# Node work of three graph convolutions and a final norm moved into the gather passes; matmul signals replaced by drains

## The reference

```python
def _gcn_conv(h, src, dst, norm, W, b, n_nodes):
    h = h @ W
    msg = h[src] * norm[:, None]          # norm = dinv[src] * dinv[dst]
    out = segment_sum(msg, dst, num_segments=n_nodes)
    return out + b
h = relu(_gcn_conv(x, src, dst, norm, W1, b1, n))
h = relu(_gcn_conv(h, src, dst, norm, W2, b2, n))
h = _gcn_conv(h, src, dst, norm, W3, b3, n)
x = layernorm(x + h)
```

## Time and profile before

| | us |
|---|---|
| median of 3 runs | 10497.17 (10493.28 to 10524.75) |
| the profiled execution | 10512.7 |
| its span | 10510.6 |

### The profile page before, as it was taken

How to read it: one execution, slowest core, us unless ns; L and a number is a source line. 1 busy time by engine, 2 the same in 40 slices (tenths; PEclk the granted TensorE clock), 3 DMA queues, 4 the chain that set the end, 5 groups by cost and what they waited for, 6 DMA issues and landing times. The chain is left out here.

```text
span 10510.6 us, 129336 instructions
## 1 busy us (share of the span) xinstructions
PE 6092.0 (58%) x27369; PEld 4863.8 (46%) x27370; DVE 4112.3 (39%) x9347; ACT 1787.8 (17%) x5309; POOL 5218.2 (50%) x5246
## 2 busy tenths in 40 slices
PE   3567666765675666667456533457854564455454
PEld 2456545644563555456334423345633443344343
DVE  5344434444453444434312523337761223224123
ACT  3222222222222222222323210001210000000000
POOL 2654454445446545644565445530036655655655
PEclk9788877877887888778778865558977787788777
DMA  5332332333233323323322145423313222222322
GB/s 149 108 94 86 98 102 84 98 90 103 83 93 103 96 85 98 105 84 89 92 82 79 32 138 165 148 97 131 114 60 88 83 71 86 85 80 72 87 78 70
DMA packets 423906, 995.27 MB, mean 95 GB/s; under 512 B 124608, under 2 KB 190016, under 8 KB 407360
## 3 DMA queue, kind: packets, MB, share of 16 engines
q0 software_dynamic: 246800, 677.71, 22.4%
q1 hardware_dynamic: 152608, 293.79, 8.5%
q10 hardware_dynamic: 24336, 22.16, 0.6%
HBM read 858.93 MB, written 134.35 MB: 95 GB/s over the span
## 5 line engine op out<-in xcount | busy, mean ns | idle before, releaser
L283 POOL DMA_INDIRECT ring<-node_table,idx x4608 | 4510.2, 979 | 3679.3 <-issue 1667.8
L250 DVE SCALAR_TENSOR_TENSOR S<-iota,block_start,dst_f 128x512 f32<-128x512 f32 x1900 | 1423.2, 749 | 3256.2 <-remote 1813.2
L497 PE MATMUL psAT<-ring,S 128*128 128x256 f32 x7600 | 2023.4, 426 | 1065.6 <-DVE AGG L614 917.8
L321 PE MATMUL psAT<-ring,S 128*128 128x256 f32 x6080 | 1709.1, 443 | 1506.2 <-DVE AGG L365 743.3
L497 PEld LDWEIGHTS psAT<-ring,S 128*128 128x128 f32 x7600 | 1599.8, 216 | 1424.0 <-DVE S L250 759.9
L321 PEld LDWEIGHTS psAT<-ring,S 128*128 128x128 f32 x6080 | 1332.8, 225 | 1878.1 <-issue 1024.0
L656 DVE TENSOR_TENSOR ring<-ring,psE 128x256 f32<-128x256 f32 x2560 | 877.0, 416 | 744.7 <-remote 358.2
L566 ACT ACTIVATE ring<-ring 128x256 f32<-128x256 f32 x2560 | 841.9, 408 | 1235.0 <-issue 651.4
L283 POOL DMA_INDIRECT ring<-att_table,idx x512 | 492.6, 962 | 471.3 <-issue 471.3
L438 PE MATMUL psE<-we_stk,stk 128*128 128x256 bf16 x2560 | 428.5, 307 | 308.4 <-DVE ring L656 156.7
L750 PE MATMUL psAT<-shared,S 128*128 128x9 f32 x1520 | 340.1, 363 | 393.1 <-DVE shared L796 310.6
(11 more groups left out here) (304 smaller groups left out, 4772.8 us busy)
## 6 DMA issues: line engine op xcount, KB each, us to landing
stk<-stack_table SPq DMA_DIRECT2D x320, 256.0 KB
ring<-node_table,idx POOLq DMA_INDIRECT x4608
rows_table<-ring SPq DMA_DIRECT2D x64, 1072.0 KB
ring<-rows_table SPq DMA_DIRECT2D x64, 1072.0 KB, 4.9
node_table<-tab ACTq DMA_DIRECT2D x136, 128.0 KB
stack_table<-stk SPq DMA_DIRECT2D x64, 256.0 KB, 2.0
node_table<-tab SPq DMA_DIRECT2D x96, 128.0 KB, 1.7
ring<-att_table,idx POOLq DMA_INDIRECT x512
```

The source lines that it names most:

```text
L250: nc.vector.scalar_tensor_tensor(S[:, 4 * g:4 * g + 4, :], iota[:, :].unsqueeze(1).to_broadcast([P, 4, P]), block_start[:, bass.ds(blk, 1) ...
L283: nc.gpsimd.indirect_dma_start(ring[:, q, 0:gw], None, table, bass.IndirectOffsetOnAxis(ap=idx[:, q:q + 1], axis=0)).then_inc(gathered[q], 16)
L321: ins = nc.tensor.matmul(psA[:, 0:D], S[:, u, :], ring[:, q, 0:D], start=(u == 0), stop=(u == U - 1))
L497: ins = nc.tensor.matmul(psA[:, 0:D], S[:, u, :], ring[:, U * ob + u, 0:D], start=(u == 0), stop=(u == U - 1))
```

## The change

- A new `conv_pass` takes the place of `edge_pass` for the three convolutions, and of the node phases of the second and third and of the closing steps and norm. The first node phase stays.
- In it `AGG` starts as a copy of `Y` (the node's own row) by ACT in place of zeros by DVE. When a second unit of an octet shows that a block is complete, then in the first two convolutions: DVE puts the block (times dinv, plus bias) into `tin`, PE turns it, ACT copies it with the relu, PE multiplies it with the next weights, DVE scales it and copies it to `tab`, ACT stores it into the other one of two tables. In the third: DVE multiplies and adds `H`, takes statistics, ACT takes the root, DVE normalises, ACT stores the block to the output. Each step works on the block that the step before it finished one border ago.
- PE's matmuls carry no signal any more in `edge_pass`, `max_pass`, the new pass, `root_pe` and `turn_weights`: a drain behind a unit (or behind a pair of turns) increments the semaphore instead, for all eight tiles at once. `octet_free` is a plain increment.
- `message_pass`, `attend_pass` and `node_phase` are as they were.

```diff
@@ edge_pass, tensor @@
-                                    ins = nc.tensor.matmul(psA[:, 0:D], S[:, u, :], ring[:, q, 0:D],
-                                                           start=(u == 0), stop=(u == U - 1))
-                                    if u % 4 == 3:
-                                        ins.then_inc(onehot_used, 4)
+                                    nc.tensor.matmul(psA[:, 0:D], S[:, u, :], ring[:, q, 0:D],
+                                                     start=(u == 0), stop=(u == U - 1))
+                                pe.drain().then_inc(onehot_used, U)
                                 pe.reg_add(npe, npe, U)
 
                             units(pe, None, cnt, unit)
-                            pe.drain().then_inc(octet_free, 1)
+                            pe.sem_inc(octet_free, 1)
@@ new: conv_pass, tensor @@
+                    def turn(m):
+                        pe.wait_ge(f_in, m)
+                        pe.wait_ge(f_copied, m)
+                        for f in range(2):
+                            nc.tensor.transpose(psT[:, P * f:P * f + P], tin[:, 0, P * f:P * f + P], ident[:, :])
+                        pe.drain().then_inc(f_turned, 1)
+                    def result(m):
+                        pe.wait_ge(f_copied, m + 1)
+                        pe.wait_ge(f_used, m)
+                        for f in range(2):
+                            nc.tensor.matmul(psO[:, 0:D], tT[:, 0, P * f:P * f + P], w[:, f, :],
+                                             start=(f == 0), stop=(f == 1))
+                        pe.drain().then_inc(f_result, 1)
...
+                            unit(True)
+                            with pe.If(cnt > 1):
+                                with pe.Fori(1, cnt):
+                                    m = pe.snap(nf_pe)
+                                    unit(False)
+                                    if not final:
+                                        turn(m)
+                                        result(m)
+                                    pe.reg_add(nf_pe, nf_pe, 1)
+                            pe.sem_inc(octet_free, 1)
@@ new: conv_pass, scalar @@
+                    def copy(m):
+                        if final:
+                            act.wait_ge(f_in, m)
+                            nc.scalar.activation(rstd[:, 0:1], mv[:, 0, 1:2],
+                                                 ACT.Sqrt, bias=eps[:, 0:1]).then_inc(f_copied, 1)
+                        else:
+                            act.wait_ge(f_turned, m + 1)
+                            nc.scalar.activation(tT[:, 0, :], psT[:, 0:D], ACT.Relu).then_inc(f_copied, 1)
+                    def move(m, b):
+                        act.wait_ge(f_tab, m)
+                        act.dma_start((out if final else tables[(n + 1) % 2])[bass.ds(b * P, P), :], tab[:, 0, 0:D]
+                                      ).then_inc(f_stored, 16)
@@ new: conv_pass, vector @@
+                    def put_in(m, b):
+                        a = block_of(AGG, b, AW)
+                        if final:
+                            nc.vector.scalar_tensor_tensor(a, a, dinv_of(b), block_of(H, b), ALU.mult, ALU.add)
+                            dve.drain()
+                            nc.vector.bn_stats(stats[:, 0, :], a)
+                            dve.drain()
+                            nc.vector.bn_aggr(mv[:, 0, :], stats[:, 0, :]).then_inc(f_in, 1)
+                        else:
+                            dve.wait_ge(f_turned, m)
+                            nc.vector.scalar_tensor_tensor(tin[:, 0, :], a, dinv_of(b), bias, ALU.mult, ALU.add
+                                                           ).then_inc(f_in, 1)
+                    def finish(m, b):
+                        if final:
+                            dve.wait_ge(f_copied, m)
+                            nc.vector.reciprocal(rstd[:, 0:1], rstd[:, 0:1])
+                            dve.drain()
+                            dve.wait_ge(f_stored, m * 16)
+                            nc.vector.tensor_scalar(tab[:, 0, 0:D], block_of(AGG, b, AW),
+                                                    mv[:, 0, 0:1], rstd[:, 0:1],
+                                                    ALU.subtract, ALU.mult).then_inc(f_tab, 1)
+                        else:
+                            dve.wait_ge(f_result, m)
+                            nc.vector.tensor_scalar(block_of(Y, b), psO[:, 0:D], dinv_of(b), None, ALU.mult
+                                                    ).then_inc(f_used, 1)
+                            dve.drain()
+                            dve.wait_ge(f_stored, m * 16)
+                            copied(tab[:, 0, 0:D], block_of(Y, b)).then_inc(f_tab, 1)
...
+                                with dve.Fori(1, cnt) as j:
+                                    m = dve.snap(nf_dve)
+                                    b = a_block(lo + j)
+                                    unit(b)
+                                    dve.drain()
+                                    finish(m, a_block(dve.snap(done_dve[0])))
+                                    put_in(m, last())
...
@@ max_pass, tensor: the same for a unit, and for both pairs of turns @@
-                            nc.tensor.transpose(psE[:, 512:512 + P], d16[:, :], ident[:, :]).then_inc(scoresT, 1)
+                            nc.tensor.transpose(psE[:, 512:512 + P], d16[:, :], ident[:, :])
+                            pe.drain().then_inc(scoresT, 1)
@@ the calls @@
-        for n in range(3):
-            node_phase(2 + n, pre_conv(n) if n else pre_h, post_conv, store=store_conv, st=1 + n,
-                       pool_post=table_conv, weights=(wa_sb, wb_sb, wa_sb)[n])
-            edge_pass(PLAIN, L + 2 + n, first_dve=add_bias if n == 2 else None,
-                      loads=third_weights if n == 0 else None)
-        on_both(...)
-        layer_norm(out.rearrange("(b p) f -> p b f", p=P))
+        node_phase(2, pre_h, post_conv, store=store_conv, st=1, pool_post=table_conv, weights=wa_sb)
+        for n in range(3):
+            conv_pass(n, L + 2 + n, conv_bias[n], (wb_sb, wa_sb, None)[n], third_weights if n == 0 else None)
```

More of the change, by code:

```diff
@@ L749, in unit @@
                                             pe.wait_ge(onehot_ready, c + u + 4)
-                                        ins = nc.tensor.matmul(psA[:, (HEADS + 1) * u:(HEADS + 1) * (u + 1)],
-                                                               S[:, u, :], picks[:, U * half + u, :],
-                                                               start=True, stop=True)
-                                        if u % 4 == 3:
-                                            ins.then_inc(onehot_used, 4)
+                                        nc.tensor.matmul(psA[:, (HEADS + 1) * u:(HEADS + 1) * (u + 1)],
+                                                         S[:, u, :], picks[:, U * half + u, :],
+                                                         start=True, stop=True)
+                                    pe.drain().then_inc(onehot_used, U)
                                     pe.reg_add(npe, npe, U)
@@ L1878, in root_pe @@
                     for f in range(2):
-                        ins = nc.tensor.transpose(psT[:, D * q + P * f:D * q + P * f + P],
-                                                  tin[:, q, P * f:P * f + P], ident[:, :])
-                ins.then_inc(root_turned, 1)
+                        nc.tensor.transpose(psT[:, D * q + P * f:D * q + P * f + P],
+                                            tin[:, q, P * f:P * f + P], ident[:, :])
+                pe.drain().then_inc(root_turned, 1)
             if ob == 2:
@@ L1887, in root_pe @@
                     for f in range(2):
-                        ins = nc.tensor.matmul(psO[:, D * q:D * q + D], tT[:, q, P * f:P * f + P], wb_sb[:, f, :],
-                                               start=(f == 0), stop=(f == 1))
-                ins.then_inc(root_done, 1)
+                        nc.tensor.matmul(psO[:, D * q:D * q + D], tT[:, q, P * f:P * f + P], wb_sb[:, f, :],
+                                         start=(f == 0), stop=(f == 1))
+                pe.drain().then_inc(root_done, 1)
         def root_act(act, i, ob):
@@ L2069, in dv @@
             return dinv[:, bass.ds(b, 1)] if not isinstance(b, int) else dinv[:, b:b + 1]
-        def pre_conv(n):
-            def pre(dve, b, q):
-                nc.vector.tensor_tensor(tin2[:, q, :], blk(AGG, b, D, AW), blk(Y, b), ALU.add)
-                dve.drain()
-                nc.vector.scalar_tensor_tensor(tin2[:, q, :], tin2[:, q, :], dv(b), conv_bias[n - 1],
-                                               ALU.mult, ALU.add)
-                dve.drain()
-                return nc.vector.tensor_scalar(tin[:, q, :], tin2[:, q, :], 0.0, None, ALU.max)
-            return pre
         def post_conv(dve, b, q):
```

131 lines of the change are left out of this document (120 added, 11 removed).

## The result

| | us |
|---|---|
| before, median of 5 | 10497.17 (10490.69 to 10528.3) |
| changed kernel, median of 5 | 10605.5 (10577.73 to 10638.98) |
| ratio | 1.0096 (95%: 1.0068 to 1.0125) |
| profiled execution, and its span | 10638.98, 10637.2 |

The account below looks back on a forecast made before the run. PE was taken to hold POOL through matmul signals up to 20 us late. 10512.7 - 165 + 2 x 45 + 5 + 2 x 10 = 10463 profiled, so 10447 us median; own range 10330 to 10585, overall 9560 to 10600.

Parts of the forecast that it names:

- Gaps: The spans without gathers between and after the convolutions: 193 us, of which 27.5 stay, so 165 us gained (150 to 175).
- Drain per unit: Five gather passes: 0.9 us more chain per unit; two-unit octet 9.4 to 11.2 us; weighted and maximum pass +10 us each.
- Turn and product: 31 borders of the first two convolutions: PE waits 2.4 us each; two-unit octet 13 us, 87 us a pass exposed without cover.
- I let it give back half of the exposed 87 us: First two convolutions: late signals shrink as a longer PE chain stops POOL more often, leaving +45 us for each.
- The forecast's own sign of being wrong: Gather passes: the forecast is wrong if a pass changes by more than some 70 us in either direction.
- The range's own terms: Whole kernel: gains of 150 to 175 us and costs of 0 to some 250, given as 10330 to 10585 us.
- The third convolution: Last gather pass: +5 us, from drains +15 net, less what the earlier bias block saves.
- the 15 us that the prediction weighed for them: 32 new table copies of a pass: 15 us if each held a gather for its own length, at most 0.48 us.
- The late signals: Finished-matmul reports in gather passes, some 280 us a pass: drains wait for the same completion, so the lateness stays but feeds back.
- A: Rival, gather passes: the drain cures the lateness, POOL then bounds the convolutions at 690 us a pass; 9622 us, chance 0.25.
- B: Rival, gather passes: the drain cures half the lateness, with one report in place of two per unit; 10027 us, chance 0.15.
- C: Rival, borders of the first two convolutions: turn and product drains are late themselves, 180 us a pass; 10720 us, chance 0.13.

## Why the prediction was wrong, by its steps

1. *Gaps*: 162 us against 165. Right; what stays is 12.3, 11.8 and 7.8 us for 9.5, 9.5 and 8.5. (The listed terms of the first 9.5 add up to 9.1.)
2. *Drain per unit*: 0.69 us a second unit and 0.4 to 0.5 an octet for a forecast 0.9 each; a two-unit octet with the drains alone takes 10.4 us, not 11.2, so the link was put too long. **For the maximum pass this step failed**: "10 us", where the pass pays 0.47 us for each of 95 units in the prompt condition and 56 us in the late one, since it ends on this chain. In the late condition it took 970, 969 and 977 us in the three traces with the old signals and 1026, 1031 and 1032 in the three with the drains. The forecast had taken the pass to end at 7008 (886 us); that is shortly after its last gather, and its last unit ends at 7096.6, 970 us from the first gather. The weighted pass was also put at 10 and grew by 55; with the old signals it took 837, 845, 853 and 873 us, with the drains 892 and 891, so 18 to 55 us are the drains'; what sets the size stays open.
3. *Turn and product*: the border takes 3.97 us for a forecast 3.6, the two-unit octet 12.8 for 13. Right in sum (the forecast's own terms, 1.8 for two drains and 2.4 for the border, would make 13.6). That "2.8 x 31 = 87 us a pass exposed if the ring gave no cover" is near the 92 and 86 measured is luck. The 87 counts what an octet takes beyond POOL's pace. Where POOL's pace does bound, in the prompt condition, the passes grew by 45 and 47; in the late one it doesn't (532 us for the last 42 octets already before, POOL's pace is 423).
4. **The main step that failed** is the next one: "I let it give back half of the exposed 87 us". In the late condition the whole addition to the chain counts, 102 us in the last 42 octets, and the lateness gave back some three tenths of it (78 and 69 us remained there), not half of a number that was already net of POOL's pace; 28 of the 31 two-unit octets stand among those 42. Two passes at 45 in place of 92 and 86 are 88 us, and the weighted and the maximum pass, at 10 in place of 55 and 56, another 91: together 179 us, where 176 lie between the forecast of 10463 for a profiled execution and its 10639. So both terms missed by about as much. The forecast's own sign of being wrong, a pass that changes by more than 70 us, came in both convolutions. (The range's own terms give 10322 to 10597, not 10330 to 10585; the measured median of 10605.5 lies above either.)
5. *The third convolution*: +7 for a forecast +5. Right, as far as can be told from one trace on each side (late traces with the old signals in it: 827, 832 and 836 us for the moved pass). Its first gather, beside the bias addition (8.67 us on DVE), takes 8.88 us here too. The new table copies hold no gather: POOL is busy 504.57 us with the 512 gathers of the first convolution after and 504.81 before, so the 15 us that the prediction weighed for them are nothing.
6. *The late signals*: "a drain waits for the same completion" was right; A and B fell (A's term for the weighted pass, 840 less 690, would be 150 and not 140), since the longest drain of a unit is 32.9 us in the first convolution and 34.4 in the third. L283's waits in the first convolution grew from 141 us (127.3 put down to PE) to 221, the way the forecast said, though under two names (last section). C named the right side, but not by its mechanism: turn and product drains are not late in the changed kernel (medians 0.41 and 1.15 us, longest 3.22 and 2.09). The Trainium skill (PSUM — Partial Sum Buffer, "Engine vs sequencer instructions") has the increment attached to the matmul itself and keeps the drain for a barrier that waits until the engine is fully idle. It gives this as a rule of correctness and no price. In the one trace that has both, attached signals were 45 to 50 us a pass cheaper beside the moved work.

Not in the sum at all was the clock. The same 1520 matmuls of the units are busy 457.5 us after and 425.45 before, 32 us more. Whether the pass is longer by as much is not shown: in the prompt condition they are busy 451.0 us in a pass of the changed kernel that takes 713.

```profile
L760 PE MATMUL psAT<-ring,S 128*128 128x256 f32 x1520 | 457.5, 467 | 341.0 <-DVE AGG L852 169.2 <-issue 111.8 <-DVE S L250 60.0
```

The unit at 8336.78 follows a unit that ran in 3.72 us and 2.44 us in which PE was idle. It starts at the lower level (granted clock 0.50, 1.2 GHz) and ends at the upper one (1.00), and takes 5.26 us in place of 3.72; the product at 8348.91 takes 2.07 in place of 1.13. Stretches of that unit and the product:

```profile
8336.80:8338.80 2.00, 2.00 (x5) 1.64 (x6) 1.50 (x4) 0.00 (x0) 1.39 (x3) 0.50 0.32 96
...
8340.40:8342.04 1.64, 1.64 (x8) 1.11 (x6) 0.00 (x0) 0.00 (x0) 1.33 (x2) 1.00 0.46 112
...
8347.70:8351.00 3.30, 2.73 (x6) 1.46 (x6) 1.75 (x3) 0.38 (x1) 0.00 (x0) 0.50 0.11 40
```

With attached signals and the product ahead, PE is busy 459.8 us with the units, turns and products together, against 512.5.

## What to carry to other kernels

Work moved out of a gap costs most of its chain (here some seven tenths) wherever the engine that receives it is the one the others wait for; a stall that seems to absorb it (here 200 us a pass of late signals and low clock) is to be tested for how much it gives back, and a margin per item is to be summed over the stretch in which the long items stand, not over the pass. A pass ends with its last unit, not with its last gather: what an edit adds to the chain behind the last gather is paid in full (45 us in the maximum pass). Keep a signal on the instruction that ends the work, give one as soon as half of a buffer is free, and issue a step that needs another engine's answer one round later.

## What the runs showed of the hardware

The reports of finished matmuls are late (drains of up to 32.9 us in the first convolution, 40.2 in the maximum pass) in one condition and not in another (no drain over 6.7 us), with the same kernel, which takes 10500 us with it and 8260 without. While they are late the cost of a change differs in size and even in sign: the changed kernel is 1.0096 of before in one and 0.9985 in the other. Why the reports are late, and what sets the condition, stays open.

A name in the idle column can mislead. In the changed kernel POOL's waits are put down to ACT's index copy (156.8 us, 22 times) and PE (63.8 us), in the version with drains and the product ahead to PE alone (222.0 us): the sums agree (220.6 and 222.0). At 8466.40 POOL is said to start on ACT's copy, but PE's product ended 1.24 us before it, just as at 8451.50, where PE is named.

```profile
L283 POOL DMA_INDIRECT ring<-node_table,idx x512 | 504.6, 985 | 371.5 <-ACT idx L267 156.8 <-issue 150.9 <-PEq L774 63.8
```
